# Attention heads on one core: 384 columns of f32 probabilities in place over the scores in PSUM, split from there by VectorE, and the loops over heads unrolled

## The reference

```python
q_hel = jnp.einsum('bshd,hed->bshe', qh, Whel) + bhel
k_hel = jnp.einsum('bshd,hed->bshe', kh, Whel) + bhel
...
helical = jnp.einsum('bhpsc,bhptc->bhst', qn, kn) / p
dot = jnp.einsum('bshd,bthd->bhst', qh, kh) / math.sqrt(hd)
attn = jax.nn.softmax(0.5 * dot + 0.5 * helical, axis=-1)
out = jnp.einsum('bhst,bthd->bshd', attn, vh).reshape(b, s, e)
```

## Time and profile before

| | before |
|---|---|
| median of 3 runs | 5,733.3 µs (5,731.94 to 5,738.86) |
| the profiled execution | 5,734.14 µs, its span 5,732.2 µs |
| granted clock, mean | 0.807 |
| busy: TensorE | 3,463.3 µs (60% of the span), 14,606 matmuls |
| busy: VectorE | 4,562.1 µs (80%) |
| busy: ScalarE | 2,952.6 µs (52%) |
| busy: GpSimd | 2,916.3 µs (51%) |
| DMA | 275.50 MB, mean 48 GB/s |

### The profile page before, as it was taken

One profiled execution on the slowest core, in us unless ns is written; L12 is line 12 of the kernel. 1 busy time (PEld: TensorE's weight loads), 2 busy tenths in 40 slices (PEclk: granted clock), 3 DMA queues, 4 the chain that ended last, 5 costly groups with the idle time before them and its releaser, 6 DMA issues. The chain is left out here.

```text
span 5732.2 us, 66648 instructions
## 1 busy us (share of the span) xinstructions
PE 3463.3 (60%) x14606; PEld 1230.7 (21%) x14606; DVE 4562.1 (80%) x8093; ACT 2952.6 (52%) x3700; POOL 2916.3 (51%) x2351
## 2 busy tenths in 40 slices
PE   7972000000000002888975899999999999999568
PEld 3330000000000001332332233333333333333123
DVE  5554776999999997553487899999999999999352
ACT  5563000101001002553445598989898988999632
POOL 1001564777777774112045366666666666666512
PEclk9996555555555556998998799999999999999889
DMA  1016324223232322000124211111111111110200
GB/s 40 11 35 119 65 25 107 64 52 66 49 66 49 66 52 76 10 14 0 58 99 166 49 35 33 32 33 33 33 32 33 32 33 34 41 37 5 80 27 30
DMA packets 143838, 275.50 MB, mean 48 GB/s; under 512 B 73808, under 2 KB 87504, under 8 KB 136336
## 3 DMA queue, kind: packets, MB, share of 16 engines
q1 hardware_dynamic: 142128, 263.57, 19.9%
q10 hardware_dynamic: 1440, 8.65, 0.4%
HBM read 178.65 MB, written 93.36 MB: 47 GB/s over the span
## 5 line engine op out<-in xcount | busy, mean ns | idle before, releaser
L1027 POOL TENSOR_TENSOR att_heads_rest<-att_heads_probs,att_heads_high 128x576 f16<-128x576 f32 x1024 | 1390.7, 1358 | 848.2 <-ACT att_heads_high L1114 842.1
L1144 DVE TENSOR_REDUCE att_heads_maxima<-att_heads_peek 128x1 f32<-128x512 f32 x2048 | 1311.2, 680 | 99.2 <-PE att_heads_peek L1040 72.2
L1112 ACT ACTIVATE att_heads_probs<-att_heads_scores 128x1024 f32<-128x1024 f32 x1024 | 1076.2, 1051 | 248.9 <-PE att_heads_scores L1058 240.6
L1058 PE MATMUL att_heads_scores<-att_heads_q,att_heads_k 128*128 128x512 f16 (+1 forms) x4096 | 1067.8, 382 | 34.2 <-issue 21.2
L1882 PE MATMUL delta_out_sums<-delta_out_squares,main_head_sum 128*128 128x512 f32 x32 | 16.6, 649 | 1763.4 <-ACT delta_out_squares L1911 1763.4
L1114 ACT ACTIVATE att_heads_high<-att_heads_scores 128x1024 f16<-128x1024 f32 x1024 | 1077.5, 1052 | 0.0
L1164 DVE TENSOR_TENSOR att_heads_rest<-att_heads_probs,att_heads_high 128x448 f16<-128x448 f32 x1024 | 892.0, 871 | 65.2 <-POOL att_heads_rest L1027 53.1
L1040 PE MATMUL att_heads_peek<-att_heads_k,att_heads_q 112*128 112x512 f16 x2048 | 687.9, 395 | 89.4 <-DVE att_heads_maxima L1144 47.5
L1761 ACT ACTIVATE delta_scan_s_terms<-delta_scan_state,delta_scan_record 128x64 f32<-128x64 f32 x256 | 104.7, 409 | 1160.2 <-DVE delta_scan_state L1818 1160.2
L1058 PEld LDWEIGHTS att_heads_scores<-att_heads_q,att_heads_k 128*128 128x128 f16 (+1 forms) x4096 | 395.0, 98 | 455.3 <-ACT att_heads_high L1114 38.8
L1074 PE MATMUL att_heads_out<-att_heads_high,att_heads_v_head 128*64 128x512 f16 x2048 | 418.5, 405 | 5.1 <-DVE att_heads_rest L1164 4.2
(11 more groups left out here) (240 smaller groups left out, 5174.0 us busy)
## 6 DMA issues: line engine op xcount, KB each, us to landing
delta_scan_record<-delta_record SPq DMA_DIRECT2D x64, 1026.0 KB, 10.7
att_heads_q<-att_hel SPq DMA_DIRECT2D x192, 128.0 KB, 3.1
att_heads_k<-att_hel SPq DMA_DIRECT2D x192, 128.0 KB, 3.3
delta_record<-delta_chunks_record SPq DMA_DIRECT2D x64, 256.5 KB, 4.7
att_hel<-att_hel_high SPq DMA_DIRECT2D x32, 512.0 KB, 3.9
att_hel<-att_hel_rest SPq DMA_DIRECT2D x32, 512.0 KB, 4.5
att_o<-att_heads_out_copy SPq DMA_DIRECT2D x256, 32.0 KB
att_out_parts<-att_o ACTq DMA_DIRECT2D x8, 1024.0 KB, 14.2
```

Source lines behind the costliest of these rows:

```text
L1027: nc.gpsimd.tensor_tensor(rest[:, step % 4, SPLIT:], probs[:, step % 4, SPLIT:], high[:, step % 4, SPLIT:], ALU.subtract).then_inc(rest_b_ ...
L1058: mm = nc.tensor.matmul(scores[:, step % 2, tokens(j)], k[0:rows, slot, number, tile * P:(tile + 1) * P], q[0:rows, slot, number, tokens(h ...
L1112: nc.scalar.activation(probs[:, step % 4], scores[:, step % 2], ACT.Exp, scale=LOGIT_SCALE).then_inc(probs_ready, 1)
L1144: nc.vector.tensor_reduce(maxima[:, m:m + 1], peek[:, m % 2], AX.X, ALU.max).then_inc(peek_read, 1)
```

## The change

- The f32 probabilities of the first 384 columns (`IN_PLACE`) no longer go to SBUF: ScalarE writes them over the scores, in PSUM, and VectorE's split reads them there. `probs` keeps the other 640 columns, which GpSimd splits. So ScalarE has three exponentials a step (1,024 columns to `high`, 640 to `probs`, 384 in place), the third after its first has ended.
- The scores' buffer is now free only when VectorE has split from it: `score(g + 3)` waits for `probs_ready` and `rest_a_ready` of step g + 1 in place of `high_ready`.
- VectorE's split no longer waits for GpSimd's.
- All loops over heads are unrolled in the program, with constant counts and no credits. 18 peeks in place of 16 are made ahead of a head (`LAST_PEEKS` 22 in place of 23), the copy of `out` stands behind 5 steps in place of 2, and `shift_rows` one step earlier.

```diff
+        IN_PLACE = 384
-        probs = s.sb("probs", [P, 4, T // 2])
+        probs = s.sb("probs", [P, 4, T // 2 - IN_PLACE])
...
-                            pool.wait_ge(high_ready, head * STEPS + step + 1 + H_CREDIT)
-                            nc.gpsimd.tensor_tensor(rest[:, step % 4, SPLIT:], probs[:, step % 4, SPLIT:], high[:, step % 4, SPLIT:],
-                                                    ALU.subtract).then_inc(rest_b_ready, 1)
+                    pool.wait_ge(probs_ready, g + 1)
+                    nc.gpsimd.tensor_tensor(rest[:, g % 4, IN_PLACE:], probs[:, g % 4], high[:, g % 4, IN_PLACE:], ALU.subtract).then_inc(rest_b_ready, 1)
...
-                    pe.wait_ge(high_ready, head * STEPS + step + 1 + H_CREDIT - 2)
+                    if g >= 2:
+                        pe.wait_ge(probs_ready, g - 1)
+                        pe.wait_ge(rest_a_ready, g - 1)
...
-                pe.sem_inc(weighed, W_CREDIT)
-                peek_scores(0, 0, range(PEEKS))
-                turn_shifts(0, 0)
-                for step in range(AHEAD):
-                    score(0, 0, step)
-                peek_scores(0, 1, range(EARLY))
-                with pe.Fori(0, QUADS - 1) as quad:
-                    for slot in range(SLOTS):
-                        attend(quad, slot, False)
+                peek_scores(range(PEEKS))
+                turn_shifts(0)
+                for g in range(AHEAD - 1):
+                    score(g)
+                peek_scores(range(PEEKS, PEEKS + EARLY))
+                score(AHEAD - 1)
+                for g in range(TOTAL):
+                    head, step = step_of(g)
+                    if g + AHEAD < TOTAL:
+                        score(g + AHEAD)
+                    if step == TURN_AT and head + 1 < BH:
+                        turn_shifts(head + 1)
+                    weigh(g)
+                    peek_scores(peeks_at(g))
...
-                    act.wait_ge(rest_a_ready, count + 1)
-                    act.wait_ge(rest_b_ready, count + 1)
-                    nc.scalar.activation(probs[:, step % 4], scores[:, step % 2], ACT.Exp, scale=LOGIT_SCALE).then_inc(probs_ready, 1)
-                    act.wait_ge(weighed, count + 1 + W_CREDIT - 4)
-                    nc.scalar.activation(high[:, step % 4], scores[:, step % 2], ACT.Exp, scale=LOGIT_SCALE).then_inc(high_ready, 1)
+                    if g >= 4:
+                        act.wait_ge(weighed, g - 3)
+                    nc.scalar.activation(high[:, g % 4], scores[:, g % 2], ACT.Exp, scale=LOGIT_SCALE).then_inc(high_ready, 1)
+                    nc.scalar.activation(probs[:, g % 4], scores[:, g % 2, IN_PLACE:], ACT.Exp, scale=LOGIT_SCALE).then_inc(probs_ready, 1)
+                    act.wait_ge(high_ready, g + 1)
+                    nc.scalar.activation(scores[:, g % 2, 0:IN_PLACE], scores[:, g % 2, 0:IN_PLACE], ACT.Exp, scale=LOGIT_SCALE).then_inc(in_place_ready, 1)
...
-                    dve.wait_ge(high_ready, head * STEPS + step + 1 + H_CREDIT)
-                    dve.wait_ge(rest_b_ready, head * STEPS + step + 1 + R_CREDIT)
-                    nc.vector.tensor_tensor(rest[:, step % 4, 0:SPLIT], probs[:, step % 4, 0:SPLIT], high[:, step % 4, 0:SPLIT],
+                    dve.wait_ge(in_place_ready, g + 1)
+                    nc.vector.tensor_tensor(rest[:, g % 4, 0:IN_PLACE], scores[:, g % 2, 0:IN_PLACE], high[:, g % 4, 0:IN_PLACE],
...
+                for g in range(TOTAL):
+                    head, step = step_of(g)
+                    if g + 1 < TOTAL:
+                        split(g + 1)
+                    read_peeks(peeks_at(g))
```

More of the change, by code:

```diff
@@ L1006, in _ @@
-                store_shift(0, 0)
-                with sp.Fori(0, QUADS - 1) as quad:
-                    for slot in range(SLOTS):
-                        follow(quad, slot, False)
-                for slot in range(SLOTS):
-                    follow(QUADS - 1, slot, True)
+                        sp.dma_start(dram["att_sum"][head:head + 1, queries], out_copy[j * WIDE + ONES:j * WIDE + V_COLS, half]).then_inc(out_stored[half], 16)
+                sp.wait_ge(ones_ready, SLOTS)
+                for head in range(SLOTS - 1):
+                    load(head)
@@ L1012, in _ @@
+                store_shift(0)
+                for head in range(BH):
+                    if head + SLOTS - 1 < BH:
+                        sp.wait_ge(scores_ready, head * STEPS + 1)
+                        load(head + SLOTS - 1)
+                    store_out(head, 0)
+                    if head + 1 < BH:
+                        store_shift(head + 1)
+                    store_out(head, 1)
                 for half in range(2):
-                    sp.wait_ge(out_stored[half], BH * 96 + 1)
+                    sp.wait_ge(out_stored[half], BH * 96)
@@ L1128, in _ @@
-                act.sem_inc(high_ready, H_CREDIT)
-                act.sem_inc(out_copied, O_CREDIT)
-                for step in range(BEFORE_COPY):
-                    powers(0, step)
-                with act.Fori(0, BH - 1) as head:
-                    turn(head, True)
-                turn(BH - 1, False)
+                for g in range(TOTAL):
+                    powers(g)
+                    if g >= QT and g % QT == BEFORE_COPY - 1:
+                        copy_out(*divmod(g // QT - 1, 2))
@@ L1146, in shifts, with read_peeks @@
[L1146 to L1152 removed]
+                def read_peeks(numbers):
+                    for n in numbers:
+                        head, m = divmod(n, PEEKS)
+                        dve.wait_ge(peek_ready, n + 1)
+                        if m == 0 and head >= 1:
+                            dve.wait_ge(max_ready, head)
+                        nc.vector.tensor_reduce(maxima[:, m:m + 1], peek[:, n % 2], AX.X, ALU.max).then_inc(peek_read, 1)
```

224 lines of the change are left out of this document (81 added, 143 removed).

## The result

| | µs |
|---|---|
| before, median of 4 runs | 5,732.6 |
| changed, median of 4 runs (8,059.1 to 8,103.6) | 8,072.9 |
| changed, the profiled execution (span 8,101.8) | 8,103.6 |
| predicted (range) | 7,680 (7,350 to 8,250) |

The ratio is 1.409, with a 95% interval of 1.405 to 1.413. The first views of the changed kernel's profile: busy time of each engine over the span, and the granted clock in 40 slices of 203 µs.

A forecast was written before the change was run, and what follows sets the result against it. The prediction took a closed wait between TensorE's scores and peeks and VectorE's split and maxima to bound the changed kernel: 983 steps × 4.10 = 4,030 µs on top of 3,650.7 gave 7,680 µs, range 7,350 to 8,250.

The forecast's parts named there:

- The ring: Heads' steps: scores wait for VectorE's split, its maxima for peeks behind those scores; 3.86 µs a step at 2.4 GHz.
- The split: VectorE's in-place split of 384 columns, one source in PSUM, one in SBUF: 0.56 µs.
- The rival that the split still stands still for GpSimd: VectorE's split stays 0.26 µs longer, at most 256 µs in all, 7,690 to 7,930 µs; chance 0.05.
- I choose a mixture, one step in six at 1.2 GHz: TensorE's clock in the heads' steps: 3.86 + 1.41/6 = 4.10 µs a step.
- the work per head: Maximum over tiles and shift row on VectorE, a transpose on TensorE: 0.7 µs × 31 = 22 µs.
- low half of the time: Rival: clock low for half the steps or more; at half, 4.57 µs a step and 8,140 µs; chance 0.10.
- The last 40 steps: Steps after peeks end early, bound by ScalarE: 1.93 µs each, 77 µs in all.
- Start and work outside the ring: Time besides the 983 steps: 3,650.7 µs, with 1 µs for more early peeks and step 0's split.
- GpSimd's 1.42 µs: GpSimd's part of a step, grown from 576 to 640 columns: 1.42 µs, hidden by ScalarE.
- the 7 stalls: Stalls at the branch behind every four heads, about 6 µs each, vanish with unrolling; already in the new sum.
- Idle before the maxima, 2,000 µs: Sign: VectorE idles before its maxima some 2.1 µs a step, 2,000 µs in all, released by TensorE's peeks.
- Engines busy about half of the stage: Sign: VectorE, ScalarE and GpSimd are busy about half of the heads' stage.

The follow-up runs named there:

- score_waits_split: Changed kernel with probabilities back in SBUF, VectorE not waiting for GpSimd, but scores still made to wait for VectorE's split: 9,055.1 µs.
- peeks_first: Changed kernel with TensorE issuing a step's two peeks ahead of scores g+3 and weighing g, not behind them: 5,581.5 µs.
- weigh_first_512: peeks_first with weighing ahead of scores, 512 columns in place, and the in-place exponential ahead of that for `probs`: 5,664.7 µs.
- fill_one: Changed kernel plus one unread matmul of 512 columns a step in TensorE's pause: 7,429.8 µs.
- unrolled_only: Changed kernel, loops still unrolled, but all f32 probabilities in SBUF and scores waiting for ScalarE alone, as before: 5,712.7 µs, ratio 0.9971.
- fill_four: Changed kernel plus four unread matmuls of 512 columns a step in TensorE's pause: 7,415.1 µs.

## Why the prediction was right, and which term was mis-sized

- *The ring, its links and their order*: right. Predicted 3.86 µs at 2.4 GHz and 5.27 at 1.2; measured 3.84 and 5.33. The links differ more than their sum: 0.14 and not 0.05 from the split to the scores (in the earlier trace rows the 0.05 was to the weights' load of a weighing), and 0.42, not 0.52, from peek to maximum. score_waits_split shows that the wait alone closes it, peeks_first that it is this ring and no other. These links are the forecast's mechanism, and they held.
- *The split*: 0.56 predicted, 547 ns measured, 692 for 512 columns in weigh_first_512 where the earlier trace rows had 691. By the Trainium skill ("VectorE: DVE Perf Modes", on the TRN2 errata) it would be 525 and 658 ns; the trace has 22 and 34 more.
- *The rival that the split still stands still for GpSimd*: out, by 1,024 splits within 24 ns. By the Trainium skill ("SBUF — State Buffer", on the shared pair) only a split with both inputs in SBUF contends; the runs agree, with 1.69 µs for one from SBUF that began with GpSimd's and 0.55 for one with a source in PSUM.
- *"I choose a mixture, one step in six at 1.2 GHz"*: this is the term that was mis-sized. The clock was low for half of the time. The mean step was 4.55 and not 4.10: 983 × 0.45 = 442 µs. The measured mean holds the work per head, for which the sum has 22 µs beside the steps, so 420 are new, and 7,680 + 420 = 8,100 is within 4 µs of the profiled 8,103.6. The rival "low half of the time", 4.57 a step and 8,140 µs, had what happened; I gave it and all beyond it 0.10. In steps, (4.55 − 0.02 − 3.84)/1.49 = 0.46 were at 1.2 GHz, 0.29 more than I chose, just inside the third that I had named as the mark of a wrong reading. That the time still lies in the range is owed to the range's upper end and not to this choice. What misled me was one case, the stretch from 3486 to 3494 µs, which I read wrongly: its high level is what stood before the fall, and not a recovery. Windows of the kernel before (columns as in the earlier trace rows):

```profile
3486.00:3488.40 2.40, 0.67 (x2) 0.10 (x1) 2.06 (x4) 2.40 (x3) 0.38 (x1) 1.00 0.16 34
3488.40:3494.00 5.60, 3.20 (x9) 0.75 (x10) 0.62 (x1) 1.31 (x3) 1.27 (x1) 0.50 0.10 23
```

And its timeline, the scores that come next:

```profile
3494.44 1.44 PE L1058 MATMUL att_heads_scores<-att_heads_q,att_heads_k 128*128 128x512 f16 x4
```

The next scores began at 1.2 GHz, straight behind the peeks, and the clock came up while they ran (1.44 µs for four, where they take 1.03 at 2.4 GHz and 1.89 at 1.2). So that piece of work was not followed by a pause, as every piece in the ring is, and it said little of the ring. That one more matmul a step holds the clock (fill_one) shows how little was missing.

- *The last 40 steps*: 1.93 predicted, copies included; measured 1.91 between two splits and 1.94 with the copies, behind the first five, in which the ring runs out. *Start and work outside the ring*: right, since 8,103.6 − 983 × 4.55 = 3,631 µs, against 3,651 − 22 = 3,629. *GpSimd's 1.42 µs*: 1.40.
- *"the 7 stalls", about 6 µs each*: six stalls, 33 µs rather than 42, and 16 in the time (unrolled_only). This didn't enter the sum.
- *Idle before the maxima, 2,000 µs*: 2,748, as the pause grows from 2.08 µs to 3.31 at 1.2 GHz. *Engines busy about half of the stage*: VectorE 39%, ScalarE 45%, GpSimd 31%, lower for the same reason. For GpSimd half didn't follow from my own terms: 1.42 of 4.10 µs are 35%.

In sum: of the 2,360 µs between unrolled_only and the changed kernel, 658 are the low clock (changed against fill_four), and 7,415 − 5,713 = 1,702 the ring at 2.4 GHz, after what the in-place split saves. peeks_first keeps that saving and has 131 µs less than unrolled_only. How much of the 131 would come from its order alone, with the probabilities in SBUF, wasn't tried; VectorE, busy all the time there, leaves little room for it.
